# Joining the halves of a triangular inverse in opposite-corner 64x64 tiles instead of 128x64 products

## The reference, cut to what matters

```
def step(S, inp):                                   # one token; S is 96 x 192 for each sequence and head
    q_t, k_t, v_t, g_t, b_t = inp
    S = S * exp(g_t)
    kv = einsum('bhk,bhkv->bhv', k_t, S)
    delta = (v_t - kv) * b_t
    S = S + einsum('bhk,bhv->bhkv', k_t, delta)
    o = einsum('bhk,bhkv->bhv', q_t, S)
o = o * rsqrt(mean(o*o) + EPS) * norm_weight * silu(gate);  x = x + o @ Wo
```

## Time and profile before

| | us |
|---|---|
| runs of the kernel, median of 3 | 2234.66 (2234.18 to 2234.72) |
| the profiled execution, its own time | 2240.87 |
| its span in the profile | 2239.1 |
| PE busy | 2133.1 (95%) |
| DVE busy | 1987.1 (89%) |
| ACT busy | 1376.2 (61%) |
| POOL busy | 1070.2 (48%) |

### The profile page before, as it was taken

One profiled execution on the slowest core, in us unless ns is written; L12 is line 12 of the kernel. 1 busy time (PEld: TensorE's weight loads), 2 busy tenths in 40 slices (PEclk: granted clock), 3 DMA queues, 4 the chain that ended last, 5 costly groups with the idle time before them and its releaser, 6 DMA issues. The chain is left out here.

```text
span 2239.1 us, 58435 instructions
## 1 busy us (share of the span) xinstructions
PE 2133.1 (95%) x21537; PEld 1488.0 (66%) x21560; DVE 1987.1 (89%) x4323; ACT 1376.2 (61%) x3891; POOL 1070.2 (48%) x1539
## 2 busy tenths in 40 slices
PE   5899999999999999999999999999999998968998
PEld 3576767677777777767777676767676765734554
DVE  8999999999999999999999999999999985467776
ACT  5566666666666666776767666666666553214665
POOL 2545453545445454545454545454545442125554
PEclk8999999999999999999999999999999999778999
DMA  5223333333333333434343433332232212140000
GB/s 142 51 69 79 79 85 79 85 83 85 85 85 85 75 88 84 92 93 94 88 93 90 94 92 93 92 76 66 66 66 52 66 38 54 28 167 7 24 20 29
DMA packets 455176, 169.16 MB, mean 76 GB/s; under 512 B 378310, under 2 KB 433894, under 8 KB 454380
## 3 DMA queue, kind: packets, MB, share of 16 engines
q1 hardware_dynamic: 454892, 165.43, 30.9%
HBM read 83.30 MB, written 56.90 MB: 63 GB/s over the span
## 5 line engine op out<-in xcount | busy, mean ns | idle before, releaser
L1493 DVE SCALAR_TENSOR_TENSOR d_y<-bank,d_cw,d_y 128x508 f32<-128x508 f32 (+2 forms) x576 | 421.3, 732 | 6.0 <-ACT d_y L1255 1.0
L852 POOL TENSOR_SCALAR d_ms<-d_sso 128x4 f32<-128x4 f32 x64 | 14.6, 228 | 532.8 <-ACT d_junk L1394 532.8
L800 POOL TENSOR_TENSOR d_Gm<-cst,gh 128x512 f16<-128x512 f32 x128 | 131.1, 1045 | 186.5 <-DVE d_ohl L1660 183.6
L1262 ACT ACTIVATE d_th<-d_y 128x512 f32<-128x512 f32 x192 | 121.2, 631 | 153.0 <-DVE d_y L1499 128.1
L1255 ACT ACTIVATE d_y<-bank,d_cw 128x512 f32<-128x512 f32 x192 | 130.8, 682 | 55.1 <-PE bank L918 49.3
L1666 DVE SCALAR_TENSOR_TENSOR x<-bank,x 128x512 f32<-128x512 f32 x128 | 87.0, 680 | 85.5 <-PE bank L1066 85.4
L835 POOL TENSOR_TENSOR d_V<-d_tok,d_kinv 128x640 f32<-128x640 f32 (+1 forms) x128 | 137.2, 1092 | 43.4 <-issue 41.3
L882 POOL TENSOR_SCALAR d_K<-d_tok,d_Em 128x96 f32<-128x96 f32 x256 | 155.5, 622 | 0.1
L1304 ACT ACTIVATE d_tok<-bank 128x384 f32<-128x384 f32 x256 | 125.7, 491 | 39.2 <-PE bank L934 35.5
L1384 ACT ACTIVATE d_Dl<-bank 128x384 f32<-128x384 f32 x128 | 62.3, 491 | 124.7 <-PE bank L1042 124.6
L1030 PE MATMUL bank<-d_wgh,hhi 128*128 128x192 f16 x1024 | 126.7, 246 | 0.0
(11 more groups left out here) (337 smaller groups left out, 6567.7 us busy)
## 6 DMA issues: line engine op xcount, KB each, us to landing
normed<-d_ohl SPq DMA_DIRECT2D x64, 384.0 KB, 3.8
lt_blocks<-d_LT SPq DMA_DIRECT2D x64, 256.0 KB, 2.9
d_fw<-turned_gate_w SPq DMA_DIRECT2D x32, 256.0 KB, 3.1
d_X<-x_blocks SPq DMA_DIRECT2D x128, 64.0 KB, 2.4
d_XT<-x_blocks SPq DMA_DIRECT2D x128, 64.0 KB, 2.5
d_fw<-turned_val_w SPq DMA_DIRECT2D x32, 256.0 KB, 3.2
d_fw<-turned_out_w SPq DMA_DIRECT2D x32, 256.0 KB, 2.8
d_st<-in_L_attn_Wg_dram SPq DMA_DIRECT2D x16, 384.0 KB, 4.2
```

The lines of the kernel that those rows point to most:

```text
L800: nc.gpsimd.tensor_tensor(Gm[:, w, :, :], over(U, 1, B), over(gh[:, w, n, :], 2, P), ALU.mult).then_inc(s["Gm_ready"], 1)
L1262: nc.scalar.activation(th[:, :, :], y[(st.p + j) % 2][:, :, :], ACT.Tanh).then_inc(s["tanh_done"], 1)
L1493: nc.vector.scalar_tensor_tensor(out=yy[:, :, tap:], in0=pp[:, :, 0:P - tap], scalar=cw[:, ds(st.kp, 1), t, 3 - tap], in1=yy[:, :, tap:], ...
```

## The change

The join is made with 64x64 tiles in opposite corners of the array. Sequences 0 and 1 use rows 0 to 63 and columns 64 to 127 in `y_join` (rows 64 to 127 and columns 0 to 63 in `x_join`); sequences 2 and 3 use the opposite corner. For this, the operands of sequences 2 and 3 have to lie in the other half of the partitions: three DMAs in each step move them, one of L issued by SP (`turned_join`), two issued by ScalarE in the middle of `copy_x64`. Around this, TensorE's order, some semaphore counts, VectorE's place of rec(4), and what GpSimd does and waits for are changed. K2 is no longer made in a head's last chunk, where nothing read it. The instructions that only raised a semaphore for a product left out are gone, and all counts are adapted (`carried(n)` counts steps with c > 0, `chained(n)` those with c < 3); of these, a few stand for all.

```
+def chained(n):
+    return n - n // CH
...
-        "YJ": sb("YJ", [P, B, HB]),
+        "YJ": sb("YJ", [P, 2, HB]),
...
+        LJ = sb("LJ", [P, 2, HB])
+        XJ = sb("XJ", [P, 2, HB])
...
+            def turned_join(n, q):                                        # SP
+                past(sp, "x21_done", n)
+                past(sp, "LT_ready", B * n + B)
+                sp.dma_start(LJ[HB:P, :, :], LT[q][0:HB, 2:B, HB:P]).then_inc(s["halves_in"], 16)
...
+                if st.recur:
+                    turned_join(st.n, st.p)
                 if st.turn:
                     gather(st)
...
                 past(pool, "tok_read", B * m + B)                         # GpSimd, values
+                past(pool, "rec_done", 13 * m + 8)
...
-                    for i in range(B):                                    # GpSimd, K2
+                    for i in range(B if c < CH - 1 else 0):
...
             def y_join(st):
                 hold(pe, s["X_ready"], 7 * st.n + 7)
-                for i in range(B):
-                    last = nc.tensor.matmul(lev[HB:P, 2 * P + i * HB:2 * P + (i + 1) * HB], LT[st.p][:, i, HB:P], X[:, 0, i, :], start=True, stop=True)
+                past(pe, "halves_in", 32 * st.n + 32)
+                for i in range(2):
+                    at = slice(2 * P + i * HB, 2 * P + (i + 1) * HB)
+                    nc.tensor.matmul(lev[HB:P, at], LT[st.p][0:HB, i, HB:P], X[0:HB, 0, i, :], start=True, stop=True)
+                    last = nc.tensor.matmul(lev[0:HB, at], LJ[HB:P, i, :], XJ[HB:P, i, :], start=True, stop=True)
                 last.then_inc(s["yps_done"], 1)
             def x_join(st):
                 hold(pe, s["Y_ready"], 2 * st.n + 2)
-                for i in range(B):
-                    last = nc.tensor.matmul(lev[0:HB, 2 * P + i * HB:2 * P + (i + 1) * HB], YJ[:, i, :], XT[:, i, HB:P], start=True, stop=True)
+                past(pe, "XTJ_in", 16 * st.n + 16)
+                for i in range(2):
+                    at = slice(3 * P + i * HB, 3 * P + (i + 1) * HB)
+                    nc.tensor.matmul(lev[0:HB, at], YJ[HB:P, i, :], XT[HB:P, i, HB:P], start=True, stop=True)
+                    last = nc.tensor.matmul(lev[HB:P, at], YJ[0:HB, i, :], XJ[0:HB, i, :], start=True, stop=True)
                 last.then_inc(s["x21_done"], 1)
...
-                if not product:                                           # pair_of
-                    pe.sem_inc(s[done], 1)
-                    return
...
-            def output(st):
+            def output(st, lo=0, hi=4):        # only the tiles lo to hi - 1
...
                     x_32(st)                                              # step, c == 0
                     proj(1, 5, 6)
-                    proj(2, 0, 6)
+                    for part in range(4):
+                        proj(2, part, 6)
+                    turn(2)
+                    proj(2, 4, 6)
+                    proj(2, 5, 6)
+                    if len(units(n)) == 1:
+                        output(st, 0, 1)
                 else:
...
                     proj(1, 5, 6)                                         # step, c > 0
+                    for part in range(5):
+                        proj(2, part, 6)
                 y_join(st)
                 if c:
-                    proj(2, 0, 6)
+                    proj(2, 5, 6)
+                if c:
+                    past(pe, "W_ready", B * carried(n) + 2)
+                    pair_of(st, "qs_done", 0, 4, lambda i: qry[0:DK, i, :], lambda i: S[:, i, :])
+                if c:
+                    turn(2)
+                elif len(units(n)) == 1:
+                    past(pe, "E_ready", n + 2)
+                    output(st, 1, 2)
+                    turn(3)
                 x_join(st)
                 past(pe, "PT_ready", n + 1)
+                if c:
+                    pair_of(st, "qs_done", 1, 7, lambda i: qry[0:DK, i, :], lambda i: S[:, i, :])
+                if c or len(units(n)) != 1:
+                    turn(3)
-                for part in range(4 if c == 0 else 2, 6):
-                    proj(2, part, 6)
-                if len(units(n)) < 2:
+                if c == 0:
+                    past(pe, "E_ready", n + 2)
+                elif len(units(n)) == 1:
                     output(st)
                 gates(st, 0)
...
-                    for h in range(2):                                    # ScalarE, copy_x64, after the copy of X
+                    for h in (1, 0):
                         r = slice(h * HB, h * HB + 32)
                         nc.scalar.activation(XT[r, :, h * HB + 32:(h + 1) * HB], ...).then_inc(s["X_ready"], 1)
+                        if h:
+                            past(a, "X_ready", 7 * n + 5)
+                            a.dma_start(XJ[HB:P, :, :], X[0:HB, 0, 2:B, :]).then_inc(s["halves_in"], 16)
+                            past(a, "X_ready", 7 * n + 6)
+                            a.dma_start(XJ[0:HB, :, :], XT[HB:P, 2:B, HB:P]).then_inc(s["XTJ_in"], 16)
...
-                    nc.scalar.activation(YJ[HB:P, :, :]..., lev[HB:P, 2 * P:], ACT.Copy)       # copy_yj
+                    nc.scalar.activation(YJ[:, :, :]..., lev[:, 2 * P:3 * P], ACT.Copy)
...
-                    nc.scalar.activation(XT[0:HB, :, HB:P], lev[0:HB, 2 * P:]..., ACT.Copy)    # join
+                    for h in range(2):
+                        last = nc.scalar.activation(XT[0:HB, 2 * h:2 * h + 2, HB:P], lev[h * HB:(h + 1) * HB, 3 * P:]..., ACT.Copy)
...
-    rec(2), rec(3), silu(st, 0), low, conv(st, 1, 1), conv(st, 1, 2), rec(4),                  # VectorE's order
+    rec(2), rec(3), silu(st, 0), rec(4), low, conv(st, 1, 1), conv(st, 1, 2),
```

More of the change, by code:

```diff
@@ L92 @@
     L_moved rec_done Xb_ready X_stored XT_stored X_loaded XT_loaded block_in
+    halves_in XTJ_in
     ks_done qs_done W_ready qs_read yps_done Y16_ready Y_ready xps_done X_ready x21_done XT_ready
@@ L1022, in gates @@
                         pe.wait_ge(s["wg_ready"], st.k + 1)
-                    past(pe, "qs_read", B * n + 2 * pair + 2)
+                    past(pe, *(("qs_read", B * carried(n) + 2 * pair + 2) if st.c else ("gate_ready", 2 * n - 1)))
                     if pair and len(units(n)) == 2:
@@ L1033, in gates, with pair_of @@
                     last.then_inc(s["gate_done"], 1)
-            def pair_of(st, done, pair, at, lhsT, rhs, rows=P, product=True):
-                if not product:
-                    pe.sem_inc(s[done], 1)
-                    return
+            def pair_of(st, done, pair, at, lhsT, rhs, rows=P):
                 for i in range(2):
@@ L1052, in output @@
                     for i in range(2):
+                        if not lo <= 2 * e + i < hi:
+                            continue
                         at = (6, 5, 7, 4)[2 * e + i]
@@ L1055, in output @@
                             past(pe, "LT_ready", B * n + 2 * B)
-                        if at == 5 and st.recur:
-                            past(pe, "W_ready", B * n + 4)
+                        if at == 5 and st.recur and st.c:
+                            past(pe, "W_ready", B * carried(n + 1))
                         if at == 7:
-                            past(pe, *(("qs_read", B * n + 4) if st.recur else ("gate_ready", 2 * n)))
+                            past(pe, *(("qs_read", B * carried(n + 1)) if st.recur and st.c else ("gate_ready", 2 * n)))
                         if at == 4:
@@ L1167, in step @@
                     proj(1, 1, 6)
-                pair_of(st, "ks_done", 0, 4, lambda i: key[:, i, :], lambda i: S[:, i, :], product=c > 0)
-                past(pe, *(("E_ready", n + 2) if st.turn else ("O_ready", 2 * n)))
-                pair_of(st, "ks_done", 1, 5, lambda i: key[:, i, :], lambda i: S[:, i, :], product=c > 0)
+                if c:
+                    pair_of(st, "ks_done", 0, 4, lambda i: key[:, i, :], lambda i: S[:, i, :])
+                    past(pe, *(("E_ready", n + 2) if st.turn else ("O_ready", 2 * n)))
+                    pair_of(st, "ks_done", 1, 5, lambda i: key[:, i, :], lambda i: S[:, i, :])
                 turn(0)
@@ L1192, in step @@
                 if c:
-                    proj(2, 0, 6)
[L1194 to L1198, removed]
-                        proj(2, part, 6)
+                    proj(2, 5, 6)
[8 more added lines that the diff above has]
+                    turn(3)
                 x_join(st)
+                past(pe, "PT_ready", n + 1)
                 if c:
-                    proj(2, 1, 6)
-                past(pe, "PT_ready", n + 1)
-                pair_of(st, "qs_done", 1, 7, lambda i: qry[0:DK, i, :], lambda i: S[:, i, :], product=c > 0)
-                turn(3)
+                    pair_of(st, "qs_done", 1, 7, lambda i: qry[0:DK, i, :], lambda i: S[:, i, :])
+                if c or len(units(n)) != 1:
+                    turn(3)
                 if n == NS - 1:
                     turn_x(1)
-                for part in range(4 if c == 0 else 2, 6):
```

(22 more changed lines are left out.)

33 lines of the change are left out of this document (18 added, 15 removed).

## The result

The changed kernel is slower: 2256.34 us (median of 4 runs, 2253.75 to 2262.22) against 2234.42 us for the kernel before, a ratio of 1.0094 with a 95% interval of 1.0080 to 1.0108. That is 22 us more, where 47 us less were forecast; it lies outside the range. The profiled execution took 2254.75 us, its span 2252.7 us (before 2240.87 and 2239.1).

What follows compares the result with a forecast made beforehand. The prediction took TensorE's instruction list as the bound, VectorE next. Its terms, -30.7 - 15 + 4 + 2 - 3 - 4 = -46.7 us, took the median from 2234.66 to 2188 us, range 2174 to 2220.

Steps and rivals of the forecast that it cites:

- part 4: ScalarE's two DMA issues, 0.8 us, up to 1.4, stay hidden; plus 2 us where cover is missing (n = 0, 4, 60).
- Part 2: TensorE's waits before `y_join` and `x_join` all go through better cover in the new order: minus 15 us, 8 to 17.
- Part 1: Opposite-corner join products overlap, so a join takes 4 slots in place of 8: minus 30.7 us, 28 to 33.
- Rival A: The 64x64 corners in the join don't overlap, so the slots save 0: 2219 us; chance 12%.
- part 6: Rec(4) ahead of `low`, `values` held back, K2 dropped: 41 us off VectorE; fewer `gate` waits, minus 4 us, 0 to 9.
- Part 3: The X copy before `y_join` lands in 2.0 us within a 2.8 us budget; 4 us allowed for waits, 0 to 58.
- Rival B: The DMA before `y_join` is late, deciding from 1.05 us in each of 48 steps; chance 12%, 8% reaching slower.
- Rival C: ScalarE's issues delay `copy_yj` for `x_join`, 0.6 us in 48 steps, giving 2217 us; some reaches VectorE through tap0(1); chance 12%.
- Part 5: Idle time put down to "issue" before turn(0) with c = 0 goes with the semaphore-only instructions: minus 3 us, 0 to 4.

Runs made afterwards that it cites:

- the kernel with the weights ahead: The changed kernel with tanh(1) ahead of `join` for c = 0, and SP loading the step's first feed-forward weights chunk ahead of `gather`: 2214.39 us, ratio 0.9909.
- the wide join and tanh(1) early: The changed kernel with the old 128-row joins, no join DMAs, and ScalarE doing tanh(1) ahead of `join` for c = 0: 2225.48 us, ratio 0.9958.
- second and third row of the last table: Kernel before with only rec(4) ahead of low and `values` held back, 2227.28 us; changed kernel with old joins and tanh(1) ahead of `join` for c = 0, 2225.48 us.
- the kernel with tanh(1) early: The changed kernel with ScalarE doing tanh(1) ahead of `join`, not behind tokens(3), in steps with c = 0: 2216.16 us, ratio 0.9913.

## Why the prediction was wrong, point by point

**The step that failed is part 4.** It follows ScalarE's queue up to `copy_yj`, asks only whether TensorE's `x_join` gets its YJ in time, and says of what stands behind `join`: "18 output passes (3.9 us) and gates(0) behind it, or gates(0) alone with c = 0: 0". That cost the delay of `join` by TensorE's list alone. ScalarE has its own list behind `join`: tokens(3), then tanh(1), with VectorE's silu(1), `add_x` and `gate` after it. "ACT has a third of its time free" was true before and is true after (195 of 300 us), and says nothing: an in-order engine with idle time is still late if it waits at the wrong place. Measured: 2.70 us in each of the steps with c = 0 (29.28 to 26.58), 40 us in the medians with the first eight steps' share. Part 2 read the new order only as cover for TensorE. Seen from ScalarE the same edit puts `x_join` off by 4.66 us in a step with c = 0 (9.17 to 13.83), and with it all that ScalarE has queued behind `join`.

**Part 1, the slots: right in mechanism and size.** A join block now lasts 0.38 us from its first start to the next block's, 0.61 with the wide join: 0.23 each, 29.4 us for 128 (forecast 30.7, 28 to 33). Two corners start 0.01 us apart, 1258.26 and 1258.27, all in bank 3. Rival A is refuted. The Trainium skill, page TensorEngine Tiling (Array Packing), Gotcha 1: PSUM Pressure, says that different row tiles cannot access the same PSUM bank at the same time; no run here shows such a limit, for 64x64 tiles no more than for the 32x32 ones of the earlier trace rows. What failed is the worth of a slot: it arrived in full with c > 0, once the weights were out of the way, and with c = 0 not at all as long as ScalarE issued the copies. The first eight steps didn't shorten either: 223.6 us before, 225.2 in the kernel with the weights ahead; nor did the three from n = 60 to 63 in that kernel (112.8 and 114.2), while with the wide join and tanh(1) early they took 105.7. The forecast had counted 0.73 us for each of these eleven, 8 us. Why they didn't wasn't looked into.

**Part 2, the waits before the joins: the sum was right, the place was not.** 10.6 us of idle time went. By the starts they were 0.61 us in a step with c = 0 (0.34 ahead of `y_join`, and 0.27 ahead of `x_join`, which part 2 had not read), 0.27 with c = 1 and nothing with c = 2 and 3: 14 us in 16 heads. Those of c = 1 went with part 6 already (29.63 to 29.39), and those of c = 0 came back in part as others. With part 6 in both and the wide join, the two orders (second and third row of the last table) differ by 0.14 us in four steps (114.63 to 114.49), 2 us in all, where 15 were forecast.

**Part 3, the copies: nearly right.** The budget of 2.8 us fits the measured 2.81, the median of the steps with c > 0 from the issue of the first copy to `y_join`. The median landing is 2.16 us for that copy (2.3 for both DMAs), 2.0 was taken, and 25 of 64 took over 2.8. The wait is 8.7 us; 4 were allowed. Rival B has the right mechanism at about a sixth of the price at which it decides, 50.7 us.

**Part 4, the issues:** 0.47 and 0.62 us, 1.1 together, inside the "up to 1.4", above the 0.8 taken from SP. ScalarE stands idle for 0.92 us at the second XT copy, because the issues stand in the same queue ahead of it. From the view of the tile XJ (ns min/median/max):

```profile
L1382 ACTq DMA_DIRECT2D d_XJ<-d_X x64: 468/479/527, 92.7 to 1943.8; - x64
L1384 ACTq DMA_DIRECT2D d_XJ<-d_XT x64: 623/627/1478, 93.2 to 1944.3; - x64
```

YJ is late for TensorE 3 times, for 1.1 us in all (`PE bank L1038 <- ACT d_YJ L1388`), at n = 0, 4 and 60. These are the steps without an output tile between the joins, for which 2 us were set: right. Rival C named ScalarE as the late engine, but put the price at `x_join` with c > 0, and kept the sign at faster. Its side remark on VectorE named tap0(1); it was tanh(1), with c = 0.

**Part 5, signals:** the 2.8 us put down to "issue" are gone from the list of waits. They can't be told from the rest.

**Part 6, rec(4)** has the size of the earlier trace rows no more. From the view of the tile XTb of the changed kernel:

```profile
L1618 DVE TENSOR_TENSOR d_XTb<-d_XTb,d_part x64: 147/148/997, 64.0 to 1904.3; 32x8 f32<-32x8 f32 x64
```

It takes 148 ns in the median, 787 before, and VectorE is busy for 80 us less, of which 38 are rec(4) (49.3 to 11.2 us in sum). With `values` held back, it brings 7.3 us; 4 was forecast, 0 to 9. In the kernel before, 62 of the 64 rec(4) met `exponents` on GpSimd and ended 0.02 us behind one of its two instructions, as the one in the earlier trace rows does; in the changed kernel 2 did, and these two took 966 and 997 ns. That a 32x8 operation with two inputs from SBUF takes five times as long while GpSimd works agrees with the Trainium skill, page SBUF — State Buffer, section "SBUF: two separate sides", by which one of the two engines holds a shared pair of ports for a whole instruction.

Taken together: forecast minus 46.7. Of this, 8 us were put on steps at both ends that don't shorten, 13 us on waits that moved or went with part 6, about 7 us on slots with c = 0 that became waits; that leaves some 19, and the kernel with tanh(1) early has 18 to 20. The shares are estimates that overlap a little, so this agreement is rough. In the changed kernel the late tanh(1) takes some 40 us more, which turns these into 22 us lost.

## What to carry to other kernels

When work is put ahead of a product, write down for each engine that waits for the product what it has queued behind that wait, and who needs that; the free share of its time is no cover. An entry moved in a second queue (here one tanh, 40 us) can make the difference between a gain and a loss, so look for the edit that a reordering needs beside it. And share out a saving by kinds of steps: a slot saved is worth nothing where the engine already waits.

## What was not expected of the hardware

- A small DMA within SBUF issued by ScalarE costs its queue 0.48 us, or 0.63, and up to 1.48; SP takes 0.51 for the same copy (320 ns for its 32 KB stores). The choice of engine hardly changes the price, only whose queue pays it.
- Such a copy of 32 KB lands in 1.8 us at best and about 2.3 in the median. The copy of X took over 2.8 us in 25 of 64 steps of the changed kernel and in 19 with tanh(1) early, and in 2 once SP's load of weights was sent earlier: landing time depends on what else is in flight, though the DMAs are busy for only 0.36 of the time.
- 64x64 products in opposite corners overlap, also when both write one bank: after the first pair, the pairs start 0.05 to 0.06 us apart, as single passes of the wide join do (0.06).
